# Halved GpSimd instructions and a double-buffered projecting stage in a cross-attention and expert layer

## The reference, cut to what matters

```python
def _L0_xattn_ref(latents, context, Wq, Wk, Wv, Wo):       # H, KV, HD = 16, 4, 96
    hidden = jnp.concatenate([context, latents], axis=1)   # 1500 + 56 rows
    q = (latents @ Wq.T).reshape(b, q_len, H, HD)
    k = (hidden @ Wk.T).reshape(b, s_len, KV, HD)
    v = (hidden @ Wv.T).reshape(b, s_len, KV, HD)
    scores = jnp.einsum('bkgqd,bksd->bkgqs', q, k) * scale
    attn = jax.nn.softmax(scores, axis=-1)
    out = jnp.einsum('bkgqs,bksd->bkgqd', attn, v)
    return out @ Wo.T
def _L0_ffn_ref(x, W_gate, b_gate, W_e, b_e):              # 8 experts, best two
    _, top_idx = jax.lax.top_k(x @ W_gate + b_gate, 2)
    y_all = jax.nn.relu(jnp.einsum('bsd,edh->bseh', x, W_e) + b_e)
    return jnp.take_along_axis(y_all, top_idx[..., None], axis=2).mean(axis=2)
x = x + _L0_xattn_ref(_layernorm(x), ctx_4096, ...)        # x (32, 56, 512), ctx (32, 1500, 512)
x = x + _L0_ffn_ref(_layernorm(x), ...)
```

## Time and profile before

| | us |
|---|---|
| median of 3 runs | 3580.04 (3578.49 to 3580.22) |
| the profiled execution, its own time | 3578.9 |
| its span on the chip | 3577.1 |
| PE busy | 3507.8 |
| DVE busy | 2141.3 |
| ACT busy | 1707.3 |
| POOL busy | 839.1 |

### The profile page before, as it was taken

How to read it: one execution, slowest core, us unless ns; L and a number is a source line. 1 busy time by engine, 2 the same in 40 slices (tenths; PEclk the granted TensorE clock), 3 DMA queues, 4 the chain that set the end, 5 groups by cost and what they waited for, 6 DMA issues and landing times. The chain is left out here.

```text
span 3577.1 us, 65292 instructions
## 1 busy us (share of the span) xinstructions
PE 3507.8 (98%) x22132; PEld 3233.4 (90%) x22132; DVE 2141.3 (60%) x3055; ACT 1707.3 (48%) x3203; POOL 839.1 (23%) x462
## 2 busy tenths in 40 slices
PE   8999999999999999999999999999999999898999
PEld 7889999999999999999999999999999999886887
DVE  5346666666666666666666666666666666655554
ACT  3225555555555555555555555555555555423222
POOL 0032222222222222222222222222222222300000
PEclk9999999999999999999999999999999999999999
DMA  6542222222222222222222222222222222353110
GB/s 218 190 133 60 61 61 61 61 61 61 61 61 61 61 60 59 61 61 61 61 60 59 60 61 61 61 61 61 61 61 61 61 61 62 92 188 116 36 35 32
DMA packets 301135, 262.29 MB, mean 73 GB/s; under 512 B 198690, under 2 KB 255394, under 8 KB 300466
## 3 DMA queue, kind: packets, MB, share of 16 engines
q1 hardware_dynamic: 301106, 261.94, 24.8%
HBM read 195.50 MB, written 66.35 MB: 73 GB/s over the span
## 5 line engine op out<-in xcount | busy, mean ns | idle before, releaser
L740 DVE TENSOR_TENSOR probs_lo<-probs,probs_hi 125x448 fp32r<-125x448 f32 (+1 forms) x896 | 697.6, 793 | 302.5 <-ACT probs_hi L667 294.4
L795 PE MATMUL ps_proj<-wv_hi,parts 128*125 128x384 f32 x3072 | 875.4, 339 | 0.0
L782 PE MATMUL ps_proj<-parts,wk_hi 128*128 128x500 f32 x2304 | 710.9, 390 | 4.7 <-DVEq L695 4.7
L795 PEld LDWEIGHTS ps_proj<-wv_hi,parts 128*125 128x125 f32 x3072 | 560.1, 186 | 4.8
L659 ACT ACTIVATE probs<-ps_scores 125x448 f32<-125x448 f32 (+1 forms) x896 | 463.0, 517 | 131.9 <-PE ps_scores L843 64.6
L135 POOL TENSOR_TENSOR parts<-raw,parts 128x1000 fp32r<-128x1000 f32 (+1 forms) x198 | 515.9, 2606 | 16.5
L795 PE MATMUL ps_proj<-wv_lo,parts 128*125 128x384 f32 x1536 | 518.5, 338 | 0.0
L782 PEld LDWEIGHTS ps_proj<-parts,wk_hi 128*128 128x128 f32 x2304 | 431.4, 188 | 92.6 <-DVEq L695 5.0
L646 ACT CAST values_hi<-ps_proj 125x384 fp32r<-125x384 f32 x384 | 184.5, 480 | 662.0 <-PE ps_proj L795 662.0
L667 ACT CAST probs_hi<-probs 125x448 fp32r<-125x448 f32 (+1 forms) x896 | 484.5, 541 | 28.4
L133 POOL TENSOR_SCALAR parts<-raw 128x1000 fp32r<-128x1000 f32 (+1 forms) x198 | 230.3, 1163 | 1015.4 <-PE ps_proj L795 828.5
(11 more groups left out here) (155 smaller groups left out, 5822.8 us busy)
## 6 DMA issues: line engine op xcount, KB each, us to landing
raw<-in_ctx SPq DMA_DIRECT2D x192, 500.0 KB, 3.6
qk_hi<-proj_out_hi SPq DMA_DIRECT2D x60, 224.0 KB, 2.0
qk_lo<-proj_out_lo SPq DMA_DIRECT2D x60, 224.0 KB, 2.2
queries_hi<-qk_hi SPq DMA_DIRECT2D x32, 336.0 KB, 3.5
queries_lo<-qk_lo SPq DMA_DIRECT2D x32, 336.0 KB, 3.6
att_raw<-attended SPq DMA_DIRECT2D x128, 84.0 KB
probs<-att_raw SPq DMA_DIRECT2D x31, 336.0 KB, 5.7
probs<-inverse_sums SPq DMA_DIRECT2D x31, 336.0 KB, 3.0
```

Source lines behind the costliest of these rows:

```text
L740: dve.tensor_tensor(prs[1][0:R, u % PRING, 0:N], pr[0:R, u % PRING, 0:N], f(prs[0][0:R, u % PRING, 0:N]), ALU.subtract).then_inc(p_lo, 1)
L782: mm = pe.matmul(pproj[n % 2][:, 0:CS], w["wk"][a][:, j // 3, i * P:(i + 1) * P], ct[v][:, c, j // 3, :], start=(j == 0), stop=(j == 3 * K ...
L795: mm = pe.matmul(pproj[n % 2][0:VT, 0:KD], ct[a][:, t // VTC, j // 3, s], w["wv"][v][:, j // 3, :], start=(j == 0), stop=(j == 3 * KT - 1))
```

## The change

Three things, of which the first is on POOL and the others are in project:

1. POOL's subtraction in `split` and its product in `normalize` become two instructions over half of the columns each, one behind the other; the second alone signals. The subtractions of L629 and L1037 and the one of L1048 stay whole.
2. `xt` has two buffers, taken in turn by the groups. ACT and DVE make their `turn` behind output 15 instead of behind output 18, and ACT's wait there is for the products of the group two back. A product waits for the last user of its own bank (`bank_free`). PE, ACT and DVE have the groups written out instead of in loops.
3. ACT has a small Sqrt ahead of its first wait for the normalization. The wait for the last stores moves from SP at the end of project to the start of attend, where SP, POOL and ACT each have it (`projections_stored`), ahead of SP's first loads, POOL's first memset and ACT's first copy.

```diff
     pool.wait_ge(stream["hi"], b * LOADS + n + 1)
-    pool.tensor_tensor(lo, raw, f(hi), ALU.subtract).then_inc(stream["lo"], 1)
+    pool.tensor_tensor(lo[:, 0:1], raw[:, 0:1], f(hi[:, 0:1]), ALU.subtract)
+    pool.tensor_tensor(lo[:, 1:2], raw[:, 1:2], f(hi[:, 1:2]), ALU.subtract).then_inc(stream["lo"], 1)
...
-    pool.tensor_tensor(home[0], home[0], home[1], ALU.mult).then_inc(stream["normalized"], 1)
+    half = H * Q // 2
+    pool.tensor_tensor(home[0][:, 0:half], home[0][:, 0:half], home[1][:, 0:half], ALU.mult)
+    pool.tensor_tensor(home[0][:, half:], home[0][:, half:], home[1][:, half:], ALU.mult).then_inc(stream["normalized"], 1)
...
-        xt = [sb(f"xt_{n}", [P, KT, GR], F32R) for n in ("hi", "lo")]
+        xt = [sb(f"xt_{n}", [P, 2, KT, GR], F32R) for n in ("hi", "lo")]
+        warm = sb("warm_p", [P, 1])
...
-                for i in range(OSLOTS):
-                    sp.wait_ge(stored[i], START + 32 * GROUPS * uses(i))
...
-                        if k == 0:
-
-                            act.wait_ge(out_done, START + g * NOUT)
-                        act.copy(xt[0][:, k, :], pt[k][:]).then_inc(xt_hi, 1)
+                        if k == 0 and g > 1:
+
+                            act.wait_ge(out_done, START + (g - 1) * NOUT)
+                        act.copy(xt[0][:, g % 2, k, :], pt[k][:]).then_inc(xt_hi, 1)
...
                 act.wait_ge(consts, 3)
+
+                act.activation(warm[:], eps[:], ACT.Sqrt)
                 norm_scale(0)
...
-                    if more:
-                        turn(g + 1)
-
-                group(0, True, first=True)
-                with act.Fori(1, GROUPS - 1) as g:
-                    group(g, True)
-                group(GROUPS - 1, False)
+                        if n == TURN_AFTER and more:
+                            turn(g + 1)
+
+                for g in range(GROUPS):
+                    group(g, g < GROUPS - 1, first=(g == 0))
...
-                    pe.wait_ge(out_lo, START + g * NOUT + max(n - OBANKS + 1, 0))
+                    pe.wait_ge(out_lo, START + bank_free(g, n))
...
+def bank_free(g, n):
+
+    last = [m for m in range(g * NOUT + n) if m % NOUT % OBANKS == n % OBANKS]
+    return last[-1] + 1 if last else 0
+
+
+def projections_stored(eng, stream):
+
+    for i in range(OSLOTS):
+        eng.wait_ge(stream["proj_stored"][i], START + 32 * GROUPS * out_uses(i))
```

More of the change, by code:

```diff
@@ L68 @@
 OSLOTS, OBANKS = 3, 4
+TURN_AFTER = NOUT - 4
 HALVES = 2 * KV
@@ L237, in project @@
         out_hi, out_lo = sem("out_hi_ready"), sem("out_lo_ready")
-        stored = [sem(f"stored{i}") for i in range(OSLOTS)]
+        stored = stream["proj_stored"]
         xg = io["x"].rearrange("(g t r) d -> g r t d", t=GT, r=RT)
@@ L245, in project @@
         w_to = [[t[:, :, cols(i)] for t in wq] for i in range(WQP)] + [[t[:] for t in w[n]] for n in ("wk", "wv")]
-        def uses(i):
-            return len(range(i, NOUT, OSLOTS))
         with nc.Block() as block:
@@ L310, in split_out @@
                     act.wait_ge(out_done, START + g * NOUT + n + 1)
-                    act.wait_ge(stored[n % OSLOTS], START + g * (32 * uses(n % OSLOTS)) + 32 * (n // OSLOTS))
+                    act.wait_ge(stored[n % OSLOTS], START + g * (32 * out_uses(n % OSLOTS)) + 32 * (n // OSLOTS))
                     R, N = (P, GR) if n < MK else (RT, KD)
@@ L382, in turn @@
                         dve.wait_ge(xt_hi, g * KT + k + 1)
-                        dve.tensor_tensor(xt[1][:, k, :], pt[k][:], f(xt[0][:, k, :]), ALU.subtract).then_inc(xt_lo, 1)
+                        dve.tensor_tensor(xt[1][:, g % 2, k, :], pt[k][:], f(xt[0][:, g % 2, k, :]), ALU.subtract).then_inc(xt_lo, 1)
                 def split_w(i):
@@ L436, in product @@
                             stat = wq[a][:, k, n * P:(n + 1) * P] if n < MQ else w["wk"][a][:, k, (n - MQ) * P:(n - MQ + 1) * P]
-                            mm = pe.matmul(po[n % OBANKS][:, :], stat, xt[b][:, k, :], start=(j == 0), stop=(j == last))
+                            mm = pe.matmul(po[n % OBANKS][:, :], stat, xt[b][:, g % 2, k, :], start=(j == 0), stop=(j == last))
                         else:
                             t = n - MK
-                            mm = pe.matmul(po[n % OBANKS][0:RT, 0:KD], xt[a][:, k, t * RT:(t + 1) * RT], w["wv"][b][:, k, :],
+                            mm = pe.matmul(po[n % OBANKS][0:RT, 0:KD], xt[a][:, g % 2, k, t * RT:(t + 1) * RT], w["wv"][b][:, k, :],
                                            start=(j == 0), stop=(j == last))
@@ L449, in group, with out_uses @@
                         product(g, n)
-                        if n == NOUT - 4 and more:
+                        if n == TURN_AFTER and more:
                             turn(g + 1)
                 turn(0)
-                with pe.Fori(0, GROUPS - 1) as g:
-                    group(g, True)
-                group(GROUPS - 1, False)
+                for g in range(GROUPS):
+                    group(g, g < GROUPS - 1)
+def out_uses(i):
+    return len(range(i, NOUT, OSLOTS))
+def bank_free(g, n):
[4 more added lines that the diff above has]
+        eng.wait_ge(stream["proj_stored"][i], START + 32 * GROUPS * out_uses(i))
 def key_part(c, i):
@@ L552, in bring_back @@
                     store_att(sp, stream, scratch, b, home)
+                projections_stored(sp, stream)
                 load_qk(0)
@@ L592, in _ @@
             def _(pool):
+                projections_stored(pool, stream)
                 for n, ap in enumerate((f(vt_hi[:, NVT]), f(vt_lo[:, NVT]), mrow[:], ident[:], own[:])):
@@ L634, in _ @@
                     act.sem_inc(s, START)
+                projections_stored(act, stream)
                 def keys(b, c, i):
@@ L1438, in build @@
             "first_hi": sem("first_rows_hi"), "first_lo": sem("first_rows_lo"),
+            "proj_stored": [sem(f"proj_stored{i}") for i in range(OSLOTS)],
             "sums_loaded": sem("sums_loaded"), "inverted": sem("sums_inverted"), "inverse_stored": sem("inverse_stored"),
```

## The result

| | before | after |
|---|---|---|
| median, us | 3579.73 (3578.49 to 3580.22, 4 runs) | 3557.12 (3555.37 to 3558.84, 4 runs) |
| ratio, 95% interval | | 0.9939 (0.9925 to 0.9953) |
| the profiled execution, its span | 3577.1 | 3553.6 |

The account below looks back on a forecast made before the run. PE, working 98% of the span, was taken as the bound, with only its idle moments to gain. The terms 0.6 + 6.1 + 1.6 + 14.9 - 0.3 gave 22.9 us, so 3557 us, range 3547 to 3569.

Parts of the forecast that it names:

- Start, 0.6: Program start: table load leaves the chain, first product starts at 14.3 instead of 14.92; gain 0.6 us, bounds 0 and 1.28.
- Group changes, 6.1: Project's three group changes: PE's waits for `xt_lo` go, with 0.1 us each for the restart; gain 6.1 us, bounds 5 and 6.3.
- Project to attend, 1.6: Between project and attend: the stores' wait no longer delays the engines' meeting; gain 1.6 us, bounds 1.2 and 1.6.
- The clock's 1.5 us: Start of attend: 1.5 us lost at the low granted clock; counted as nothing, kept as a bound.
- The batches, 14.9: Attend's 31 batches: halves remove PE's wait for `probs_lo`; 0.48 us each, gain 14.9 us, lower bound 7, upper 19.2.
- I take the middle: Batches: between 0.34 us gained with a new late wait and 0.62 without it, 0.48 a batch was taken.
- First issued, first served: Batches, rival: POOL takes every turn, a second wait replaces part of the first; 10.5 for 14.9 us, 3561.5 in all; chance 0.25.
- The walk: One batch: POOL's halves and DVE's instructions timed in turn; all in time but the last, a new wait of 0.2 us.
- The last batch, -0.3: End of attend: splits end some 2.5 us later, L629 at 3102.7 sets combine; loss 0.3 us, bounds loss 2, gain 2.8.
- The wait only moves: Batches, rival: DVE loses its spare time and PE pays later; only project's 8.0 us stay, 3572; chance 0.11.
- Slower: Third pair (L137, L138), rival: each half holds DVE about as long as the whole did; 3610 us; chance 0.04.
- It doesn't do what it says: Project, rival: ACT is late for output 16, PE misses a bank, group changes keep half their 6.1 us; 3560; chance 0.05.

Follow-up runs that it names:

- the variant with four parts: The changed kernel with each split subtraction in four parts of 250 columns instead of two halves: 3551.14 us, ratio 0.9925.
- the 900 columns: The changed kernel with each split subtraction in two instructions of 900 and 100 columns instead of 500 and 500: 3562.81 us, ratio 0.9954.
- the last version: The changed kernel with only the third pair of pieces split, in four parts, all else whole, and combine's first rows subtracted on VectorE: 3547.21 us, ratio 0.9914.

## Why the prediction was right, point by point

Predicted were 22.9 us and a time of 3557.0; measured 22.6 and 3557.1. The nearness is partly luck. The terms of the sum measured 0.8, 5.4, 1.8, 12.6 and -0.4 in the trace, together 20.3 where 22.9 were forecast. What made up for it is the clock, which the sum had at nothing: 1.2 us in the first product and 1.7 in batch 0 of the profiled execution. No variant had as much in the first product, and one of ten had it in batch 0. The mis-sized term is that of the batches.

**Start, 0.6.** 0.81 to the first product, and 0.53 between the variant without the small Sqrt and the changed kernel. The Sqrt's share is the 0.53, for the other 0.3 us come from mean and variance, which were there at 7.87 us instead of 8.17 with and without it. What I had not counted is how fast the first product then runs: 2.53 us instead of 3.77, since the clock rose at 13.7 us instead of 17.6. I put that down to chance: in variants with the same start it rose between 14.0 and 19.7.

**Group changes, 6.1.** Right: 5.4 us for the rest of project in the table. The term's 0.1 us each for the restart was not there: the three changes themselves went from 2.03, 2.11 and 2.19 us from start to start to 0.18 each, 5.8 less in all, and the group behind each now takes 0.1 us longer, not shorter.

**Project to attend, 1.6.** Right: 1.82, and 2.4 when only this wait is put back. The clock's 1.5 us, kept as a bound, came in the profiled execution (batch 0 gained 2.1 us, of which 0.4 are a batch's own share), and in one more variant; the other nine showed a granted clock of 0.5 in the first microseconds of attend.

**The batches, 14.9.** The mechanism was right and the size off. POOL's halves in the earlier trace rows moved by 11.76 us were walked to end at 457.36, 458.97, 460.64, 462.25 and 463.86 and DVE behind them at 464.35; they ended, moved alike, at 457.37, 458.98, 460.65, 462.24, 463.86 and 464.34. What failed is the step "I take the middle": I let DVE pass one of POOL's halves in half of the batches, and none was passed: the late unit is there in each of the batches 1 to 30. That is the outcome of the rival "First issued, first served". The new wait cost 0.25 us by the variant with four parts, so what was left was 0.407 x 31 = 12.6 us. The rival's price of 10.5 was too low because its own wait was put at 0.28 with a first wait of 0.62; the two together measured 0.65.

The Trainium skill, SBUF — State Buffer, section Who interferes with whom, says that such a VectorE instruction and a GpSimd one exclude each other for the whole instruction, whoever issues first. In the batch after, the trace agrees at POOL's four halves and disagrees at its tensor_scalar of 447.19, as it did at 459.90 before. POOL stood ready, and this one came later and ran at its full speed, as at the same place of every batch:

```profile
447.39 0.61 DVE L757 TENSOR_TENSOR probs_lo<-probs,probs_hi 125x448 fp32r<-125x448 f32 x1
```

POOL's took 1.70 us instead of 1.03. The walk had this passing in it. So the runs settle that the hold is as long as the piece (the 900 columns), and leave open who gets the next turn.

**The last batch, -0.3.** -0.37. POOL's splits ended 2.86 us later, of 2.5 estimated, and PE was done 6.5 us earlier for nothing, as foreseen. The variants show the chain behind it: POOL's last split, the load of the first rows, their hi and lo, and combine 0.8 us behind. What the prediction read wrongly is the kernel before: L629 didn't set combine there. It ended 3.2 us before combine, and PE's last product, 2.68 us late behind L629 itself, ended last. That is why the halves' delay of 2.8 us cost only 0.4.

**The other rivals.** *The wait only moves* and *Slower* would need a half of about 1.8 us; it took 1.24 to 1.27 where nothing stood against it and 1.38 to 1.45 on average. *It doesn't do what it says* in project: ACT is not late; PE goes on after 0.17 us. There is no new releaser of PE there.

## What to carry to other kernels

Where two engines block each other over SBUF, it is the length of the single instruction that the other one waits for. Cutting it helps at the places where something short of time stands behind the victim, and costs everywhere else; here two pieces in six gave all of the gain. Cutting the rest delayed POOL's end by 2.9 us with halves and 4.3 with four parts, and the next stage by 0.5 and 2.2. And look at starts, not at the list of waits alone: a quarter of a microsecond in each of 31 batches, 7 us, was in no wait of the view.

At a stage's end, ask for the chain that releases the next stage before removing waits from the busiest engine. PE was done 6.5 us earlier in the last batch and nothing was gained by it. There were two chains of nearly the same length, PE's and that of the first rows, and only the version that shortened both, with Wo whole and the subtraction on VectorE, started combine 3.6 us sooner than the changed kernel.

## What the runs showed of the hardware

The granted clock does not follow from the pause alone. In the variant with halves only, it fell after 1.86 us of idle PE between two groups, to 1.2 GHz:

```profile
163.00:166.40 3.40, 3.40 (x10) 2.98 (x10) 0.45 (x2) 0.54 (x1) 0.00 (x0) 0.50 0.53 170
...
161.72 0.45 PE L441 MATMUL ps_out<-xt_hi,wq_hi 128*128 128x448 f32 x1 [1.86 <-DVE xt_lo L387]
```

In the kernel before the same pauses left it high, and in the changed kernel so did 2.86 us, after which other variants lost it. It can also fall when PE is already back at work: in the last version attend began at 203.81 with its matmuls 0.22 us apart, and from 204.9 to 208.3 they came 0.42 apart. The start of attend at half the clock cost batch 0 of the kernel before some 1.7 us against that of the changed one (the 2.1 of the table less a batch's share), and combine and experts, which no edit changes behind the first rows, took 471.9 to 476.6 us. So one profile can't decide a term of 1 to 3 us. How much of the 3 to 5 us between runs of one kernel is the clock's, and what decides it, no run here shows.

A subtraction on GpSimd that nothing hinders takes 1.24 to 1.27 us for 500 columns, 1.29 for 512 and 2.29 for 1000, and 0.72 for the 250 of the four parts, so cutting one in two costs about 0.2 us.
